# First pass: three dummy products behind each group's gate products, two narrow products less, maxima in another PSUM bank

## What is computed

```python
# block 1, per sequence of 64 tokens and per head
log_f = log_sigmoid(fg); cs = concat([0, cumsum(log_f)])
log_d = where(tri, (cs - cs.T)[1:, 1:] + ig.T, neg)
m = max(log_d, axis=-1)                    # the "maxima"
d = exp(log_d - m)
c = q @ (k.T / sqrt(dh)) * d
n = maximum(sum(c, axis=-1), exp(-m))
h = c / (n + eps) @ v
# block 2, routing to one of 8 experts
idx = argmax(softmax(x @ wg)); mask1 = one_hot(idx)
locations1 = cumsum(mask1, axis=0) - 1.0   # place of a token in its expert
...
```

## Time and profile before

| what | value |
|---|---|
| median of 3 runs | 569.85 us (569.83 to 570.12) |
| the profiled execution, its own time | 571.48 us |
| its span, first to last instruction | 569.7 us |
| mean granted clock of TensorE | 0.88 |
| PE busy over the span | 506.6 us, 89% |
| DVE, ACT, POOL busy | 59%, 54%, 38% |

### The profile page before, as it was taken

One profiled execution on the slowest core, in us unless ns is written; L12 is line 12 of the kernel. 1 busy time (PEld: TensorE's weight loads), 2 busy tenths in 40 slices (PEclk: granted clock), 3 DMA queues, 4 the chain that ended last, 5 costly groups with the idle time before them and its releaser, 6 DMA issues. The chain is left out here.

```text
span 569.7 us, 13049 instructions
## 1 busy us (share of the span) xinstructions
PE 506.6 (89%) x3926; PEld 366.2 (64%) x3926; DVE 333.4 (59%) x1455; ACT 306.9 (54%) x764; POOL 217.3 (38%) x210
## 2 busy tenths in 40 slices
PE   3589999999999999998889999999975788888886
PEld 2566787887777778774437777777732356656563
DVE  6345788877877778688423223333112677877873
ACT  4666666656666656422123333333204578888873
POOL 4301124434444445466700000000058888888500
PEclk9997778778777767698789999999995999999999
DMA  4973112222222111140121444443143556666621
GB/s 119 224 197 86 58 58 76 77 76 76 74 74 74 56 35 40 40 130 24 51 68 45 112 112 111 111 111 93 38 110 37 113 108 144 135 145 144 138 76 55
DMA packets 85068, 52.00 MB, mean 91 GB/s; under 512 B 7555, under 2 KB 78886, under 8 KB 85030
## 3 DMA queue, kind: packets, MB, share of 16 engines
q1 hardware_dynamic: 73766, 43.09, 27.7%
q0 software_dynamic: 11264, 8.43, 8.6%
HBM read 26.07 MB, written 16.91 MB: 75 GB/s over the span
## 5 line engine op out<-in xcount | busy, mean ns | idle before, releaser
L692 POOL DMA_INDIRECT s_xs<-slots_y,s_gidx x64 | 98.8, 1544 | 152.5 <-DMA slots_y<-s_ye 133.2
L822 ACT ACTIVATE s_ht<-heads,s_cols 128x512 f32<-128x512 f32 x64 | 44.0, 687 | 82.7 <-PE heads L1079 82.4
L147 ACT ACTIVATE s_xn<-s_xs,s_ln_shift,s_ln_rstd 128x128 f32 (+1 forms) x192 | 77.6, 481 | 15.6 <-DVE s_ln_shift L140 15.5
L669 POOL DMA_INDIRECT slots_x<-s_xn,s_sidx x56 | 55.1, 984 | 56.8 <-DVE s_sidx L1376 44.0
L99 DVE BATCH_NORM_STATS2 s_ln_stats<-s_xs 128x6 f32 (+1 forms) x256 | 54.5, 279 | 25.8 <-DMA s_xs<-slots_y,s_gidx 20.3
L1079 PE MATMUL heads<-s_xet,s_w_sb 128*128 128x512 f32 x128 | 59.4, 608 | 1.7 <-DVE s_xet L1456 1.7
L1086 PE MATMUL bank<-s_w_sb,s_ht 128*128 128x128 f32 x512 | 59.9, 275 | 0.9 <-DVE s_ye L1465 0.9
L1086 PEld LDWEIGHTS bank<-s_w_sb,s_ht 128*128 128x128 f32 x512 | 58.5, 192 | 1.5 <-issue 1.5
L656 POOL TENSOR_TENSOR s_hs<-s_hs,s_head_w 128x512 f32<-128x512 f32 x16 | 20.3, 1268 | 95.4 <-DVE s_hs L1337 95.4
L968 PE MATMUL heads<-s_dec_r,s_dec_l 128*128 128x512 f32 x64 | 52.5, 970 | 1.7 <-DMA s_dec_r<-s_mrow 1.7
L911 PE MATMUL bank<-s_ones_b 128*128 128x512 bf16 x187 | 50.4, 410 | 0.0
(11 more groups left out here) (195 smaller groups left out, 954.2 us busy)
## 6 DMA issues: line engine op xcount, KB each, us to landing
slots_x<-s_xe SPq DMA_DIRECT2D x8, 516.0 KB, 7.8
s_xe<-slots_x SPq DMA_DIRECT2D x16, 258.0 KB, 3.2
s_xs<-in_x_dram SPq DMA_DIRECT2D x16, 256.0 KB, 3.0
s_ctxb<-in_ctx_dram SPq DMA_DIRECT2D x16, 256.0 KB, 3.2
s_kpt<-s_kt SPq DMA_DIRECT2D x16, 256.0 KB, 2.7
s_w_sb<-in_L_ffn_w_dram SPq DMA_DIRECT2D x16, 256.0 KB, 3.3
slots_y<-s_ye SPq DMA_DIRECT2D x16, 256.0 KB, 2.3
s_ctxv<-in_ctx_dram SPq DMA_DIRECT2D x16, 256.0 KB, 3.5
```

The lines of the kernel that those rows point to most:

```text
L147: last = act.activation(out(t), tile(t), ACT.Identity, bias=self.shift[:, j:j + 1], scale=self.rstd[:, j:j + 1])
L669: pool.indirect_dma_start(out=slots_x, out_offset=bass.IndirectOffsetOnAxis(ap=slots_of(g, q)[:, t:t + 1], axis=0), in_=routed(g)[:, q, t, ...
L692: pool.indirect_dma_start(out=xs[:, n * D:(n + 1) * D], out_offset=None, in_=slots_y, in_offset=bass.IndirectOffsetOnAxis(ap=gidx[:, n:n + ...
L822: act.activation(ht[:, s_par, c, :], heads[:, c, :], ACT.Gelu_apprx_tanh, bias=col).then_inc(h_done, 1)
```

## The change

The maxima go into bank 7, where the logits and the counts are, and F is no longer formed a second time: DVE copies F from PSUM to SBUF (`fsum`) behind `a_values`, and a new DVE step `token_maxima` adds it to the turned maxima (`mtok`). ACT's `exp_m` reads `mtok` and stands right before `decays` in its list. The counts of earlier groups are kept on all 128 partitions (`upto`) and are added by DVE in `find_places`, so that the product L1025 goes as well. On PE `count_tokens` now stands ahead of `turn_maxima`, and behind the gate products of groups 2 to 15 `keep_clock(1, 3)` issues three products of 512 columns into bank 1.

```diff
         cap = sb("cap", [P, S])
         prio = sb("prio", [P, E])
         prio_i = sb("prio_i", [P, E], I32)
-        ones_f = sb("ones_f", [1, P])
-        carry = sb("carry", [1, 2, E])
-        carry_i = sb("carry_i", [1, E], I32)
+        upto = sb("upto", [P, 2, GT + 1, E])
+        upto_i = sb("upto_i", [P, E], I32)
         reset = sb("reset", [R, P])
         kqkv = sb("kqkv", [P, 3, 2 * NH])
...
                 act.activation(softp[:, :], eneg[:, :], ACT.Ln, bias=1.0).then_inc(gate_act, 1)
 
             def exp_m(g, half, q):
-                act.wait_ge(mt_ps, g + 1)
+                act.wait_ge(mtok_done, g + 1)
                 need(act, n_done, g - 1)
-                act.activation(em[:, q, :], bank[6][:, 256:256 + R], ACT.Exp, scale=-1.0).then_inc(em_done, 1)
+                act.activation(em[:, q, :], mtok[:, :], ACT.Exp, scale=-1.0).then_inc(em_done, 1)
 
             def decays(g, half, q):
...
                     values(*two)
                 if one:
                     keys(*one)
-                if two:
-                    exp_m(*two)
                 if six:
                     routed_exp(*six)
...
                 if five:
                     routed_rows(*five)
                 if two:
+                    exp_m(*two)
                     decays(*two)
                 if zero:
...
                 if isinstance(g, int) and g == 0:
                     pe.wait_ge(dve_setup, 1)
                 pe.wait_ge(kt_done, g + 1)
-                hold(pe, em_done, g, consts)
+                hold(pe, a_done, g, consts)
                 pe.wait_ge(qt_done, g + 1)
                 for t in range(GT):
...
                 pe.matmul(bank[6][:, 64:64 + R], tri[:, :], logf[:, :], start=True, stop=True).then_inc(f_ps, 1)
 
             def turn_a(g, half, q):
-                pe.wait_ge(a_done, g + 1)
+                pe.wait_ge(fsum_done, g + 1)
                 pe.transpose(bank[6][0:R, 128:256], am[:, q, :], ident[:, :]).then_inc(at_ps, 1)
 
             def turn_maxima(g, half, q):
                 hold(pe, mrow_done, g + 1, consts)
-                pe.matmul(bank[6][:, 256:256 + R], tri[:, :], logf[:, :], start=True, stop=False)
-                pe.matmul(bank[6][:, 256:256 + R], mrow[:, q, :], ident[0:R, 0:R], start=False, stop=True).then_inc(mt_ps, 1)
+                pe.matmul(bank[7][:, 256:256 + R], mrow[:, q, :], ident[0:R, 0:R], start=True, stop=True).then_inc(mt_ps, 1)
 
             def decay_exponents(g, half, q):
...
                     pe.wait_ge(late_in, 16 * len(late_loads))
                 pe.wait_ge(xt2_done, g + 1)
                 need(pe, cum_used, g)
+                pe.wait_ge(mtok_done, min(g + 4, NG) if isinstance(g, int) else g + 4)
                 for t in range(GT):
                     last = pe.matmul(bank[7][:, t * E:(t + 1) * E], xt2[:, t * P:(t + 1) * P], wg_sb[:, :],
...
                 cum = bank[7][:, 128:128 + W]
                 pe.matmul(cum, tri_b[:, :], onehot[:, :, :].rearrange("p t e -> p (t e)"), start=True, stop=False)
                 for t in range(GT):
-                    pe.matmul(cum[:, (t + 1) * E:W], ones_b[:, :],
-                              onehot[:, t:t + 1, :].to_broadcast([P, GT - t, E]), start=False, stop=False)
-                pe.matmul(cum, ones_f[:, :], carry[:, q:q + 1, :].to_broadcast([1, GT + 1, E]),
-                          start=False, stop=True).then_inc(cum_ps, 1)
+                    last = pe.matmul(cum[:, (t + 1) * E:W], ones_b[:, :],
+                                     onehot[:, t:t + 1, :].to_broadcast([P, GT - t, E]), start=False, stop=(t == GT - 1))
+                last.then_inc(cum_ps, 1)
 
             def while_idle(at, n):
...
                 zero, one, two, three, _, five, six = at
                 if three:
                     scores(*three)
-                if two:
-                    turn_maxima(*two)
                 if six:
                     while_idle(at, 4)
                     count_tokens(*six)
+                if two:
+                    turn_maxima(*two)
                 if one:
                     gate_products(*one)
+                    if not isinstance(one[0], int) or one[0] >= 2:
+                        keep_clock(1, 3)
                 if three:
                     head_values(*three)
...
                         down(s - 1, (j - 1) % 2, ((j - 1) % 4) // 2)
 
             need(pe, hs_done, NG)
-            need(pe, em_done, NG)
+            need(pe, a_done, NG)
             keep_clock(6, 12)
             turn_slots(0, 0, 0)
...
             def log_forget(g, half, q):
 
                 dve.wait_ge(gate_act, nth(g, 2, 2))
-                need(dve, mt_ps, g)
+                need(dve, f_ps, g)
                 dve.scalar_tensor_tensor(out=logf[:, :], in0=gates[:, 1, :], scalar=0.0, in1=softp[:, :],
                                          op0=ALU.min, op1=ALU.subtract).then_inc(gate_steps, 1)
...
                 dve.wait_ge(f_ps, g + 1)
                 need(dve, at_ps, g - 1)
                 dve.tensor_tensor(am[:, q, :], gates[:, 0, :], bank[6][:, 64:64 + R], ALU.subtract).then_inc(a_done, 1)
+                dve.tensor_copy(fsum[:, :], bank[6][:, 64:64 + R]).then_inc(fsum_done, 1)
 
             def running_max(g, half, q):
...
                 if not isinstance(g, int) or g >= 2:
                     dve.wait_ge(m_in[q], half * 32)
                 dve.tensor_tensor_scan(mrow[:, q, :], reset[:, :], bank[6][0:R, 128:256], 0.0, ALU.add, ALU.max).then_inc(mrow_done, 1)
+
+            def token_maxima(g, half, q):
+                dve.wait_ge(mt_ps, g + 1)
+                need(dve, em_done, g)
+                hold(dve, fsum_done, g + 1, consts)
+                dve.tensor_tensor(mtok[:, :], bank[7][:, 256:256 + R], fsum[:, :], ALU.add).then_inc(mtok_done, 1)
 
             def decayed_scores(g, q, u):
...
 
                 dve.wait_ge(cum_ps, g + 1)
                 cum = bank[7][:, 128:128 + (GT + 1) * E].rearrange("p (t e) -> p t e", e=E)
-                dve.tensor_tensor(own[:, :, :], cum[:, 0:GT, :], onehot[:, 0:GT, :], ALU.mult).then_inc(slot_steps, 1)
-                dve.tensor_copy(carry[:, 1 - q, :], cum[0:1, GT, :]).then_inc(cum_used, 1)
+                dve.tensor_tensor(upto[:, q, :, :], cum, upto[:, 1 - q, GT:GT + 1, :].to_broadcast([P, GT + 1, E]),
+                                  ALU.add).then_inc(cum_used, 1)
+                hold(dve, cum_used, g + 1, consts)
+                dve.tensor_tensor(own[:, :, :], upto[:, q, 0:GT, :], onehot[:, 0:GT, :], ALU.mult).then_inc(slot_steps, 1)
                 dve.wait_ge(slot_steps, g + 1)
                 need(dve, place_copied, g - 1)
...
                 if five:
                     ln2.dve_newton(dve, five[0], [(0, five[0])])
                     norm2(*five)
+                if two:
+                    token_maxima(*two)
                 if one:
                     gate_values(*one)
```

More of the change, by code:

```diff
@@ L262, in flamingo @@
         mrow = sb("mrow", [R, 2, P])
+        fsum = sb("fsum", [P, R])
+        mtok = sb("mtok", [P, R])
         em = sb("em", [P, 2, R])
@@ L345, in flamingo @@
         mt_ps = sem("mt_ps")
+        fsum_done = sem("fsum_done")
+        mtok_done = sem("mtok_done")
         em_done = sem("em_done")
@@ L440, in one_row @@
             return v.rearrange("(a n) -> a n", a=1)
-        IDENT_AT, ROWS_AT, TRI_AT, CONSTS = 2, 5, 7, 30
+        IDENT_AT, ROWS_AT, TRI_AT, CONSTS = 2, 5, 7, 29
         block = ctx.enter_context(nc.Block())
@@ L645, in _ @@
             step(pool.iota(prio_i[:, :], pattern=[[-1, E]], base=E, channel_multiplier=0))
-            step(pool.memset(ones_f[:, :], 1.0))
             step(pool.memset(nsq_bias[:, :], 1e-9))
-            step(pool.iota(carry_i[:, :], pattern=[[N, E]], base=-1, channel_multiplier=0))
+            step(pool.iota(upto_i[:, :], pattern=[[N, E]], base=-1, channel_multiplier=0))
             step(pool.tensor_copy(prio[:, :], prio_i[:, :]))
-            step(pool.tensor_copy(carry[:, 0, :], carry_i[:, :]))
+            step(pool.tensor_copy(upto[:, 1, GT, :], upto_i[:, :]))
             assert done == CONSTS
```

## The result

| | before | changed |
|---|---|---|
| median | 570.12 us (569.83 to 572.62, 5 runs) | 580.41 us (579.34 to 589.56, 5 runs) |
| ratio, with its 95% interval | | 1.017 [1.014, 1.020] |
| the profiled execution / its span | 571.48 / 569.7 us | 589.56 / 587.8 us |
| mean granted clock | 0.88 | 0.87 |

The change costs 10.3 us; 8.9 were forecast (578.8 against 569.9). The ratios leave out runs more than 1.5% above the quickest of the same kernel, which here cuts into a kernel's own spread, so the medians in this text are of all runs. The profiled execution of the changed kernel is the longest of its five: it shows more of the loss than the median has.

The account below looks back on a forecast made before the run. PE, at a mean clock of 0.75, was taken to set the step length in steps 3 to 16. 10.5 - 1.5 - 0.5 + 0.4 = +8.9 us gave 580.4 for the profiled execution, 578.8 us median; range 569 to 588.

Parts of the forecast that it names:

- Where the time would go: Steps 3 to 16 alone: mean clock within 0.72 to 0.78, head values over 3 us in most; later passes unchanged.
- DVE's cover: DVE's 16.4 us of waits for PE at `a_values` in eight steps, expected to hide some 0.4 us added a step.
- Dummies: 42 extra products ahead of the head values in steps 3 to 16, on PE's path: +10.5 us.
- rival C: Low-clock stretches grow; half of the ten short steps go from 14.39 to 16.67 us: 11 us more, 590 us, 14%.
- The bounds, 9.1 and 18: Price of the 42 extra products in steps 3 to 16: 9.1 us at the high clock, 18 at the low.
- Two products less: L957 and L1025 gone from PE: 1.5 us won in ten short steps, 0.5 us in the last five.
- DVE's +0.4: The copy of F between `a_values` and the next one-hot choice adds 0.1 us in four first steps: 0.4 us.
- B: Low-clock stretches in steps 3 to 16 shrink by what the dummies cost, some 18 us less: 570 us, 11%.
- D: DVE's added work shows; PE waits at the one-hot choice in all steps: +5.6 us, 584 us, 7%.
- Rival A: Dummies hold the clock up through the head values in steps 3 to 16: 20 us off, 559 us, 13%.
- The full gain: Transposes and wide products also run at the high clock in steps 3 to 16: 534 us, 3%.
- the forecast by that rule: Dummies in a stream without gaps repair nothing, only their high-clock price is paid: +7.5 us, 577.4 us.

## Why the prediction was right in its sum, and not in its terms

**Where the time would go: right.** Steps 3 to 16 and nothing else; the clock falls in the narrow gate products with TensorE busy; the mean clock stays in 0.72 to 0.78 (0.72); head values over 3 us in most steps (14 of 14); DVE's cover holds. Gate products start 2.8 us after the scores in short steps and 3.8 in long ones: 3.10 and 3.85 us, so the long step was met and the short one missed. The choice ends later in the short steps as well (TensorE waits 0.62 us for it in step 13, where 0.05 was reckoned), and what the two products gave back shrank.

**"Dummies", +10.5: too low in the traced run, and its main reason fell.** That the low stretches keep their length and only the high price is paid holds in step 12 and not in step 13. In the traced run steps 12 and 13 have 17.4 x 2 x 0.29 + 16.7 x 2 x 0.31 = 20.4 us at the low clock (10.1 and 10.3), 17.2 before (10.3 and 6.9): the short step became like the long one, 16.67 us, as rival C had it, and so did the other three short steps of the loop; steps 4 and 6 grew by 2.1 us each. That makes six of the ten short steps, where C reckoned with five. That rival was given 14% and 590 us; the run at 589.56 is it. The other runs lie between 579 and 581, where C may hold in part; they have no trace. Between medians three dummies cost 18.4 us on chip C, 8.5 and 14.7 on chip A (with the new order and with the old). The bounds, 9.1 and 18, are met within a microsecond at both ends; the value within them was taken too near the lower one for the traced run and for chip C.

**"Two products less", -2.0, with DVE's +0.4: too small where the clock plays along.** The kernel without dummies is 9.7 us faster than before on chip C, 4.8 on chip B, 2.9 slower on chip A; -1.6 was reckoned. The product time itself was sized well: 0.2 us a step where two traces are alike. What was missed is that a shorter step also moves the place where the clock falls. In the trace of chip C the account gives 5.5 us of the gain in steps 3 to 16 (5.9 measured) to the low-clock time. Why this comes out otherwise on chip A is not settled. In steps 3 to 16 its trace has 2.6 us more idle time of TensorE than that of chip C (14.0 against 11.4), and 7 us more at the low clock (98 against 91); the late increments are there as well, but no run separates them.

So on chip C the two errors, 8 us too little gain and 8 us too little loss, cancel, and the sum, +8.9, is met by +8.7. That the sum comes out so well is luck. Both terms were read off steps whose low-clock time was held nearly fixed; that it moves, and by how much, is the term that was left out, though rivals B and C named it.

**Rivals B and D.** B's shrinking low time didn't come in the first trace (125 us for 102). In the trace of chip C, of that kernel's quickest run, it nearly did: 87 us, 15 less, where B wanted 18; the steps still took 1.9 us more. D's cause is absent, since DVE waits 17.0 us where it waited 16.4. Its sign is there all the same: TensorE waits for the choice in every step.

**Rival A, the dummies hold the clock: wrong for three, right for six.** The text had named what spoke against it, "there are twelve dummies around the same head values there; here three". Six fast head values in fourteen were to decide; three dummies gave none or a few (0 in the first trace, 3 and 2 later), six gave 10 of 14 in the profiled run of chip C and 6 of 14 in that of chip B. The full gain was priced too high at 534 us: with DVE as the bound at 12.9 us a step, 14 x 12.9 = 181 us are only 24 less than 204.8, which gives 546. Neither is reached: the steps of the loop stop at 13.2 and 13.9 us, bound by waits between DVE, ACT and TensorE, and in steps 4 to 7 the clock falls all the same (four head values of 3.63 us with six). No run went below 556 us.

**A fall without idle gaps.** The head values' clock rises from 0.50 to 1.00 in a stream that had next to no idle time, when products of full width are added: the row of step 13 with six dummies stands beside the earlier trace rows. The Trainium skill, "TensorE: Matmul & The Clock Gate", section "HAM oscillation — how this bites in real kernels", asks for no idle gaps. The trace shows a fall where there were none; the forecast by that rule, 577.4 us for three dummies, can't be told from 578.8 by a kernel whose runs spread over ten microseconds, but for six it would have given 9 us more than for three, and they took 13 less.

## What to carry to other kernels

A dummy product pays only where there are enough of them. In this kernel three in a group didn't come back: in steps 12 and 13 of the first trace they ran at the low clock's price, and in step 13 more of the work behind them fell into the low stretch; six and nine held the clock in most steps of their traces on chip C. So try none, a few and many on one chip before judging; here 0, 3, 6 and 9 gave 562, 581, 568 and 562 us. And where a change shortens or lengthens a step whose clock oscillates, add a term for the low-clock time, which may be larger than the change itself, and widen the range by the spread of the runs; the best kernel found simply leaves the dummies out and keeps the two products less, with nine dummies its equal.

## What the runs showed of the hardware that was not expected

- The clock falls with TensorE busy: in step 13 of the changed kernel it goes in the gate products at 198.57, 1.7 us after the counts began and with no pause since; the only idle time in that step is the 0.62 us ahead of them. The 3.6 us of quarter-array head values then stay at 0.50.
- One kernel's runs on one chip spread from 560.8 to 581.3 us (six dummies), where the kernel before spreads over 6.6 us. Step 6 of that program took 12.5 us in one traced run and 16.9 in another.
- One chip (A) delivered TensorE's semaphore increments in bursts, up to 4.5 us behind the recorded end of the products, by a trace that also lacks some of these events, and a comparison made on it (1.004 for the kernel without dummies) differed from the others' (0.987 and 0.980).
